# Adding shifted products on TensorE in 32 by 32 tiles instead of on GpSimd

## The chip, the cores and the metric

The kernel runs on one core of one Trainium2 chip. The metric is the device time of one execution in microseconds (us), lower is better; the median of the runs is compared. A profile is of one execution. Engines by the names of the profile: PE is TensorE, DVE is VectorE, ACT is ScalarE, POOL is GpSimd, SP issues the DMAs. PEld is PE's loading of weights.

## What is computed

An input x of 8 batches, 128 channels and 16 x 16 points, all float32, goes through two residual blocks, each after a group normalisation (groups of 4 channels over all points):

```python
x = x + L0(gn(x), w_qkv, w_gate, b_gate)      # dilated 3x3 neighbourhood attention
x = x + L1(gn(x), W_qkv, b_qkv, W_proj, b_proj)   # attention between channels
```

L0 splits q, k and v (128 channels each) into four units of 32 channels (two heads of 16), with dilations 1, 2, 4 and 8. For each point and head:

```python
kp, vp = unfold3x3(k, dil), unfold3x3(v, dil)      # nine shifted copies, zeros outside
attn = softmax(einsum('bhdn,bhdkn->bhnk', qh, kp) * scale)
out  = einsum('bhnk,bhdkn->bnhd', attn, vp)        # sum over the nine neighbours
```

Each unit's output is scaled by a gate, a softmax over the four units of a projection of the mean of each channel. L1 projects to p, takes softmax(p p^T) between the 32 channels of each of four heads over the 256 points, applies it to p, projects again and adds biases.

## The kernel before

**Halves and layout.** The eight batches are worked on in two halves (`ph` 0 and 1; batches 0, 2, 4, 6 and 1, 3, 5, 7) of four batches each. In L0 the 128 partitions of a tile hold one unit (32 channels) of all four batches of a half: partitions 32j to 32j+31 are batch j of the half. In L1, and in the input, the partitions are the 128 channels of one batch. So the result of L0 has to be brought from "one unit, four batches" into "one batch, four units". This is `restore`.

**First block.** PE projects q, k and v. DVE multiplies q by the shifted k (`multiply_qk`), PE sums over the channels of a head (`sum_scores`), DVE and ACT make the softmax, and `prob` holds the nine weights for each head and point. PE copies them to all channels of their head in `spread(ph, s, chunk)`, into two PSUM buffers in turn (banks 0 and 1, or 2 and 3): four products with 64 rows and 128 columns of weights. DVE multiplies them by the shifted v in `multiply_pv(ph, s, chunk)` and writes to `pv[s]`, nine slots of 256 points; slot 3*ci+ri belongs to column shift ci and row shift ri, slot 4 is the centre. A chunk is one column shift, in the order centre, left, right, with three row shifts each. At the image's edge a product covers fewer than 16 x 16 points: for dilation 8 a shift along one axis leaves 128 points, along both axes 64. For units 2 and 3 the centre product goes to `acc[:, ph, s, :]` instead of `pv`.

`spread` of a chunk waits until DVE has multiplied the chunk two before it (`pv_ready`), since it writes the same banks. `multiply_pv` waits for its `spread`, and in the second half for the additions of the first half's same unit to be done, since it overwrites `pv[s]`.

**Adding.** Eight additions in a tree make one sum out of a unit's nine products, in `acc` (`additions`, `operands`). POOL makes those of the first half's four units and of the second half's units 0 and 1 (`POOL_SUMS = (ND, 2)`, line 340), and counts them on `added`. DVE makes those of the second half's units 2 and 3 (`add_neighbours`, line 625), and counts on `dve_added`. POOL works its queue in the written order. Between its additions of the second half stand two roots (`rsqrt`, line 305): `rsqrt(2)` (for group 0) behind the fifth addition of unit 0, `rsqrt(3)` (for group 1) behind the first addition of unit 1. The order is in `RSQRT_AFTER`. Each waits for DVE's variance.

**Restoring and the second norm.** Batches are taken in four groups of two: groups 0 and 1 are the first half, 2 and 3 the second. `restore(g)` waits until all additions of its half are done and makes for each of two batches four products with columns of the identity: all 128 partitions in, 32 columns of weights, 256 points, one unit out to partitions 32s to 32s+31 of the bank of the batch (banks 4 and 5, 6 and 7, 0 and 1, 2 and 3 for groups 0 to 3). DVE adds x in `first_residual(g)` (line 632), which gives the channel sums too; ACT squares (`squares`), PE sums over a group of channels (`group_stats`), DVE makes the variance (`second_variance`, lines 513 to 516: `gst`, `gsq`, `gvar`), POOL the root, DVE the bias (`second_norm_bias`, line 522, `nbias`), and ACT (groups 0 and 1) or DVE (groups 2 and 3) normalises. Then comes L1, group by group.

**Order.** Each engine works through one list of calls written out by hand. Around the change PE's list is `spread` (1, 0, 0) to (1, 1, 0), `restore(0)`, `spread` (1, 1, 1), `group_stats(0)`, `restore(1)`, `spread` (1, 1, 2), `group_stats(1)` (lines 966 to 974). DVE's is (1, 0, 0) to (1, 1, 0), `first_residual(0)`, (1, 1, 1), `second_variance(0)`, `first_residual(1)`, (1, 1, 2), `second_variance(1)`, (1, 2, 0), (1, 2, 1), both biases, (1, 2, 2), (1, 3, 0), additions of unit 2, (1, 3, 1), (1, 3, 2), additions of unit 3, `attention_shift` of groups 0 and 1, `first_residual(2)` (lines 714 to 735). At the end of the second half PE runs `restore(2)` and `restore(3)` (lines 995 and 996). `keep_clock(n)` issues n products that nobody reads.

All matrix products go through the helper on line 763. One float32 product shows up in the profile as two MATMULs and two LDWEIGHTS.

Of the kernel before, what the change touches and what calls it, by code (L numbers as in the profile page):

```python
# [6 lines left out]
B, H, W = 8, 16, 16  # L7
# [23 lines left out]
NORM_ON_DVE = (2, 3)  # L31
POOL_SUMS = (ND, 2)

# [14 lines left out]
def columns(d, ci):  # L48

    co = (ci - 1) * d  # L50
    return max(0, -co), min(W, W - co), co
# [33 lines left out]
def valid_rows(s, ri):  # L85
    if PAD[s]:
        return 0, H
    ro = (ri - 1) * DIL[s]
    return max(0, -ro), min(H, H - ro)
# [8 lines left out]
def build(nc, x, wpack, consts, selc, out):  # L98
    with ExitStack() as ctx:  # L99
# [143 lines left out]
        def of_phase(ph):  # L243
            return slice(ph, B, PHASES)

        def operands(ph, s, n, target, slot):
# [245 lines left out]
        def _(dve):  # L492
# [103 lines left out]
            def multiply_pv(ph, s, chunk):  # L596
# [5 lines left out]
                dve.wait_ge(spread_ready, c + 1)  # L602
                if ph and chunk == 0:
                    dve.wait_ge(added, ADDS * (s + 1))
                c0, c1, co = columns(DIL[s], ci)
                nc_ = c1 - c0
                for n, ri, dri, r0, dr, a0, da, rows in pieces(s):
                    o = view(pv[s], (3 * ci + ri) * N + r0 * W + c0, [[dri * N + dr * W, n], [W, rows], [1, nc_]])
                    if ci == 1 and n == 1:
                        o = view(acc, (ph * ND + s) * N, [[W, rows], [1, nc_]])  # L610
                    a = view(ps, 1024 * (c % 2) + 64 * r0 + W * ri + c0, [[W * dri + 64 * dr, n], [64, rows], [1, nc_]])
                    b = view(v[s], (ph * ROWS[s] + a0) * W + c0 + co, [[da * W, n], [W, rows], [1, nc_]])
                    last = nc.vector.tensor_tensor(o, a, b, ALU.mult)  # L613
                last.then_inc(pv_ready, 1)

            def add_neighbours(ph, s):

                done = ADDS * (s - POOL_SUMS[ph])
                for n, (target, slot, after) in enumerate(additions(s)):
# [94 lines left out]
            for i in range(3):  # L714
                multiply_pv(1, 0, i)
            multiply_pv(1, 1, 0)
            first_residual(0)
            multiply_pv(1, 1, 1)
            second_variance(0)
            first_residual(1)  # L720
            multiply_pv(1, 1, 2)
# [39 lines left out]
        def _(pe):  # L761
            def mm(o, w, m, start=True, stop=True):
                return nc.tensor.matmul(o, w, m, start=start, stop=stop)  # L763
# [98 lines left out]

            def restore(g):

                ph, first = g // 2, GB * (g % 2)
                if g % 2 == 0:
                    pe.wait_ge(added, ADDS * sum(POOL_SUMS[:ph + 1]))
                    if POOL_SUMS[ph] < ND:
                        pe.wait_ge(dve_added, ADDS * (ND - POOL_SUMS[ph]))
                if ph == 0:  # L870
                    pe.wait_ge(shift_ready, g + 1)
                    pe.wait_ge(qk_ready, ND * PHASES)
                if g == 2:
                    pe.wait_ge(pv_ready, 12 * PHASES)
                for i in range(GB):
                    for s in range(ND):
                        last = mm(ps[32 * s:32 * s + 32, BANK[g] + i, 0:N],
                                  ident[:, 32 * (first + i):32 * (first + i) + 32], acc[:, ph, s, :])
                    last.then_inc(restored, 1)

# [84 lines left out]
            keep_clock(6)  # L965
            for i in range(3):
                spread(1, 0, i)
            spread(1, 1, 0)
            restore(0)
            spread(1, 1, 1)  # L970
            group_stats(0)
            restore(1)
            spread(1, 1, 2)
# [20 lines left out]
            keep_clock(3, BANK[2])  # L994
            restore(2)
            restore(3)
            fuse(0, 0)
# [65 lines left out]
```

## Time and profile before

| | us |
|---|---|
| three runs | 84.91, 84.68, 84.34 |
| median | 84.68 |
| the profiled execution's own time | 84.39 |
| its span, first to last instruction | 82.6 |

The times of a run contain the span and a constant part around it. The page gives for each engine how long it was busy and in which fortieth of the span; the chain that ended last, followed back from the last instruction; and the groups of instructions with their counts and durations. MATMULs are pipelined: a record is longer than the distance to the next one, so how long a piece of PE's work keeps the engine is read from starts, not from the sum of records. An instruction of DVE or POOL likewise overlaps the one before it by a few hundredths of a us.

### The profile page before, as it was taken

What the parts mean: (1) busy time and instruction counts of PE and PEld (TensorE: products, weight loads), DVE (VectorE), ACT (ScalarE), POOL (GpSimd) and SP (SyncE); (2) the same over time, 40 slices, a digit from 0 to 9 for tenths busy, and PEclk for the clock granted to TensorE, in tenths of its full rate; (3) what the DMA queues carried; (4) which work ended last, traced back from release to release, by engine and by line L of the source; (5) the groups of instructions that cost most, each with busy time, mean ns of one, the idle gap of its engine ahead of it and who ended that gap; (6) DMA issues with size and microseconds to landing.
All of it is one profiled execution on the core that took longest, in us unless ns stands there. A gap on an engine that the chain in (4) does not pass through costs nothing.

```text
span 82.6 us, 2228 instructions
## 1 busy us (share of the span) xinstructions
PE 67.3 (81%) x888; PEld 49.0 (59%) x888; DVE 69.6 (84%) x191; ACT 30.7 (37%) x97; POOL 42.4 (51%) x82
## 2 busy tenths in 40 slices
PE   0099899799867979999966797979999787999960
PEld 0099695476433656686855664667685545677830
DVE  1087679999999999999999698889999999857980
ACT  4396599615537000000030004220993155485320
POOL 7104279108700009999999999899990003300000
PEclk9999999999999999999999999999999999999999
DMA  0995004000000000000000000000000000011244
GB/s 5 315 356 150 1 0 100 5 0 0 8 0 0 4 12 0 0 0 0 12 0 0 0 0 0 0 8 0 0 0 0 0 8 4 0 63 64 71 158 159
DMA packets 3019, 3.11 MB, mean 38 GB/s; under 512 B 320, under 2 KB 2752, under 8 KB 3008
## 3 DMA queue, kind: packets, MB, share of 16 engines
q1 hardware_dynamic: 2576, 2.69, 9.9%
q10 hardware_dynamic: 432, 0.26, 1.4%
q8 instruction: 7, 0.11, 0.6%
q14 instruction: 4, 0.03, 0.1%
HBM read 1.91 MB, written 1.05 MB: 36 GB/s over the span
## 4 chain that ended last, share of the span: by engine, by line
DVE 42%; POOL 29%; PE 13%; issue 5%; DMA 4%; ACT 2%; POOLq 1%; ACTq 0%
DVE qk L572 17%; POOL acc L340 13%; POOL pv L340 12%; PE ps L763 11%; DVE pv L613 5%; DMA xt<-x_dram 4%; POOL rstd L305 4%; DVE acc L625 4%; DVE pv L625 3%; DVE x L632 2%; PE ps L898 2%; DVE ssum L589 1%; ACT pT L402 1%; DVE x L658 1%; POOLq L99 1%
## 5 line engine op out<-in xcount | busy, mean ns | idle before, releaser
L763 PE MATMUL ps<-prob,sel 64*128 64x192 f32 (+6 forms) x192 | 17.7, 313 | 2.9 <-DVE pv L613 1.9
L613 DVE TENSOR_TENSOR pv<-ps,v 128x128 f32<-128x128 f32 (+7 forms) x32 | 17.1, 569 | 1.7 <-PE ps L763 0.9
L763 PE MATMUL ps<-xn,wp 128*32 128x256 f32 (+1 forms) x208 | 16.4, 382 | 1.7 <-DVE shifted L582 1.2
L763 PEld LDWEIGHTS ps<-prob,sel 64*128 64x128 f32 x192 | 13.7, 186 | 6.9 <-DVE pv L613 4.8
L340 POOL TENSOR_TENSOR pv<-pv 128x240 f32<-128x240 f32 (+3 forms) x24 | 14.6, 617 | 0.1
L572 DVE TENSOR_TENSOR qk<-q,k 128x720 f32<-128x720 f32 (+7 forms) x24 | 13.9, 646 | 0.1
L763 PE MATMUL ps<-xt 128*128 128x128 f32 x56 | 10.6, 334 | 4.1 <-DMA xt<-x_dram 4.1
L763 PEld LDWEIGHTS ps<-xn,wp 128*32 128x32 f32 (+1 forms) x208 | 9.7, 116 | 6.3 <-DVE shifted L582 1.7
L340 POOL TENSOR_TENSOR acc<-acc,pv 128x256 f32<-128x256 f32 (+4 forms) x20 | 12.6, 635 | 0.5
L305 POOL TENSOR_TENSOR rstd<-gvar,mhalf 128x2 f32<-128x2 f32 (+1 forms) x6 | 4.9, 824 | 14.9 <-DVE gvar L516 14.9
L763 PEld LDWEIGHTS ps<-xt 128*128 128x128 f32 x56 | 8.6, 230 | 5.2 <-DMA xt<-x_dram 4.1
L763 PE MATMUL ps<-qk,cs 128*32 128x192 f32 (+6 forms) x176 | 7.8, 302 | 0.9 <-ACT v L385 0.5
L340 POOL TENSOR_TENSOR acc<-pv 128x256 f32<-128x256 f32 x4 | 2.9, 728 | 8.5 <-DVE pv L613 8.5
L395 ACT ACTIVATE expd<-shifted 128x576 f32<-128x576 f32 x2 | 1.4, 684 | 15.8 <-DVE shifted L582 15.8
L402 ACT ACTIVATE pT<-x 128x256 f32<-128x256 f32 x8 | 3.3, 411 | 10.4 <-DVE x L632 10.4
L763 PEld LDWEIGHTS ps<-qk,cs 128*32 128x32 f32 x176 | 4.7, 109 | 3.6 <-ACT v L385 1.0
L541 DVE TENSOR_REDUCE sums<-xt 128x1 f32<-128x256 f32 x8 | 2.8, 413 | 2.8 <-DMA xt<-x_dram 2.8
L763 PE MATMUL ps<-p,mT 128*128 128x256 f32 x16 | 4.6, 399 | 0.3 <-ACT mT L429 0.2
L763 PE MATMUL ps<-acc,cs 128*32 128x256 f32 x64 | 4.1, 383 | 0.7 <-issue 0.6
L360 ACT ACTIVATE xn<-xt 128x256 f32<-128x256 f32 x8 | 3.2, 404 | 2.0 <-DMA xt<-x_dram 2.0
L415 ACT ACTIVATE p<-ps,wp 128x256 f32<-128x256 f32 x8 | 3.4, 473 | 1.1 <-PE ps L763 1.1
L572 DVE TENSOR_TENSOR qk<-ps,k 128x128 f32<-128x128 f32 (+4 forms) x12 | 3.8, 379 | 0.0
(75 smaller groups left out, 94.0 us busy)
## 6 DMA issues: line engine op xcount, KB each, us to landing
xt<-x_dram SPq DMA_DIRECT2D x4, 256.0 KB, 3.6
out_dram<-x SPq DMA_DIRECT2D x8, 128.0 KB, 1.8
wp<-wpack_dram SPq DMA_DIRECT2D x1, 325.0 KB, 5.6
sel<-selc_dram SPq DMA_DIRECT2D x4, 64.0 KB, 3.9
cs<-consts_dram ACTq DMA_DIRECT2D x1, 130.0 KB, 3.3
cs<-consts_dram ACTq DMA_DIRECT2D x2, 64.0 KB, 2.6
```

Of the source, the lines that this page charges most:

```text
L305: nc.gpsimd.tensor_tensor(rstd[:, bs], gvar[:, bs], mhalf[:, bs], ALU.pow).then_inc(rstd_ready, 1)
L340: nc.gpsimd.tensor_tensor(o, a, b, ALU.add).then_inc(added, 1)
L360: nc.scalar.activation(xn1[:, b // GB, b % GB, :], xt[:, b, :], ACT.Square, accum_out=sums[:, b, 1:2]).then_inc(square_ready, 1)
L402: nc.scalar.activation(pT[:, g, 2 * i:2 * i + 2, :].rearrange("p t n -> p (t n)"), x1[:, b, :], ACT.Square, accum_out=sums1[:, b, 1:2]).th ...
L415: nc.scalar.activation(p1[:, g, i, :], ps[:, BANK[g] + i, 0:N], ACT.Identity, bias=wp[:, W_B1:W_B1 + 1]).then_inc(p1_copied, 1)
L541: nc.vector.tensor_reduce(sums[:, b, 0:1], xt[:, b, :], AX.X, ALU.add).then_inc(sum_ready, 1)
L572: last = nc.vector.tensor_tensor(o, a, b, ALU.mult)
L613: last = nc.vector.tensor_tensor(o, a, b, ALU.mult)
L625: nc.vector.tensor_tensor(o, a, b, ALU.add).then_inc(dve_added, 1)
L632: nc.vector.scalar_tensor_tensor(out=x1[:, b, :], in0=ps[:, BANK[g] + i, 0:N], scalar=1.0, in1=xt[:, b, :], op0=ALU.mult, op1=ALU.add, acc ...
L763: return nc.tensor.matmul(o, w, m, start=start, stop=stop)
L898: last = nc.tensor.transpose(ps[:, BANK[g] + i, P * t:P * t + P], p1[:, g, i, P * t:P * t + P], ident)
```

## The change

`POOL_SUMS` becomes (3, 2) and `TENSOR_SUMS = ((3,), ())`: nobody adds the first half's unit 3 in SBUF any more. `restore` is replaced by `sum_units(ph, units)`. It works in tiles of 32 rows and 32 columns: for each unit s and each batch j of the half, the product of a 32 x 32 identity with partitions 32j to 32j+31 goes to partitions 32s to 32s+31 of the bank of batch j. For a unit that is already added that is one product of 256 points for each batch, from `acc`. For the first half's unit 3 it is nine for each batch, one for each neighbour straight from `pv[3]`, over the points that the neighbour covers, accumulated in PSUM. All four banks of a half are filled by one call; `restored` counts a batch when its last unit in the order of issue has its last product.

PE's list has `sum_units(0, (3,))` between `spread` (1, 0, 1) and (1, 0, 2), `sum_units(0, (0, 1, 2))` behind (1, 0, 2), then `spread` (1, 1, 0) and (1, 1, 1), `group_stats(0)`, `spread` (1, 1, 2), `group_stats(1)`; and for the second half `sum_units(1, (0, 1, 2, 3))` in place of the two `restore`. DVE's list has `first_residual(0)` ahead of (1, 1, 0) and `first_residual(1)` ahead of (1, 1, 1). The first half's unit 3 has its centre product in `pv[3]`, and the second half's multiply of unit 3 waits for all four batches to be restored.

```diff
--- before.py
+++ after.py
@@ -29,7 +29,8 @@
 GROUPS = B // GB
 NORM_ON_ACT = (4, 6, 1, 3, 5, 7)
 NORM_ON_DVE = (2, 3)
-POOL_SUMS = (ND, 2)
+POOL_SUMS = (3, 2)
+TENSOR_SUMS = ((3,), ())
 
 RSQRT_AFTER = ((1, 0, 4), (1, 1, 0))
 
@@ -243,6 +244,15 @@
         def of_phase(ph):
             return slice(ph, B, PHASES)
 
+        def neighbours(s):
+
+            return [(3 * ci + ri, *valid_rows(s, ri), *columns(DIL[s], ci)[:2])
+                    for ci in CENTRE_FIRST for ri in CENTRE_FIRST]
+
+        def added_before(ph, s):
+
+            return len([u for u in range(POOL_SUMS[ph], s) if u not in TENSOR_SUMS[ph]])
+
         def operands(ph, s, n, target, slot):
 
             ci, ri = divmod(slot, 3)
@@ -600,13 +610,15 @@
                 if chunk == 0:
                     dve.wait_ge(proj_copied, tiles.index((2, s, ph)) + 1)
                 dve.wait_ge(spread_ready, c + 1)
-                if ph and chunk == 0:
+                if ph and chunk == 0 and s in TENSOR_SUMS[0]:
+                    dve.wait_ge(restored, SLOTS)
+                elif ph and chunk == 0:
                     dve.wait_ge(added, ADDS * (s + 1))
                 c0, c1, co = columns(DIL[s], ci)
                 nc_ = c1 - c0
                 for n, ri, dri, r0, dr, a0, da, rows in pieces(s):
                     o = view(pv[s], (3 * ci + ri) * N + r0 * W + c0, [[dri * N + dr * W, n], [W, rows], [1, nc_]])
-                    if ci == 1 and n == 1:
+                    if ci == 1 and n == 1 and s not in TENSOR_SUMS[ph]:
                         o = view(acc, (ph * ND + s) * N, [[W, rows], [1, nc_]])
                     a = view(ps, 1024 * (c % 2) + 64 * r0 + W * ri + c0, [[W * dri + 64 * dr, n], [64, rows], [1, nc_]])
                     b = view(v[s], (ph * ROWS[s] + a0) * W + c0 + co, [[da * W, n], [W, rows], [1, nc_]])
@@ -615,7 +627,7 @@
 
             def add_neighbours(ph, s):
 
-                done = ADDS * (s - POOL_SUMS[ph])
+                done = ADDS * added_before(ph, s)
                 for n, (target, slot, after) in enumerate(additions(s)):
                     if n == 0 or ADD_NEEDS[n] > ADD_NEEDS[n - 1]:
                         dve.wait_ge(pv_ready, 12 * ph + 3 * s + ADD_NEEDS[n])
@@ -713,11 +725,11 @@
             multiply_pv(0, 3, 2)
             for i in range(3):
                 multiply_pv(1, 0, i)
+            first_residual(0)
             multiply_pv(1, 1, 0)
-            first_residual(0)
+            first_residual(1)
             multiply_pv(1, 1, 1)
             second_variance(0)
-            first_residual(1)
             multiply_pv(1, 1, 2)
             second_variance(1)
             for i in range(2):
@@ -860,23 +872,37 @@
                     last = mm(o, sel[half:half + 64, j % 2, s, :], m)
                 last.then_inc(spread_ready, 1)
 
-            def restore(g):
-
-                ph, first = g // 2, GB * (g % 2)
-                if g % 2 == 0:
-                    pe.wait_ge(added, ADDS * sum(POOL_SUMS[:ph + 1]))
-                    if POOL_SUMS[ph] < ND:
-                        pe.wait_ge(dve_added, ADDS * (ND - POOL_SUMS[ph]))
+            def sum_units(ph, units):
+
                 if ph == 0:
-                    pe.wait_ge(shift_ready, g + 1)
+                    pe.wait_ge(shift_ready, PHASES)
                     pe.wait_ge(qk_ready, ND * PHASES)
-                if g == 2:
+                else:
                     pe.wait_ge(pv_ready, 12 * PHASES)
-                for i in range(GB):
-                    for s in range(ND):
-                        last = mm(ps[32 * s:32 * s + 32, BANK[g] + i, 0:N],
-                                  ident[:, 32 * (first + i):32 * (first + i) + 32], acc[:, ph, s, :])
-                    last.then_inc(restored, 1)
+                parts = []
+                for s in units:
+                    if s in TENSOR_SUMS[ph]:
+                        pe.wait_ge(pv_ready, 12 * ph + 3 * s + 3)
+                        parts.append([(pv[s], slot * N, r0, r1, c0, c1) for slot, r0, r1, c0, c1 in neighbours(s)])
+                        continue
+                    if s < POOL_SUMS[ph]:
+                        pe.wait_ge(added, ADDS * (sum(POOL_SUMS[:ph]) + s + 1))
+                    else:
+                        pe.wait_ge(dve_added, ADDS * (added_before(ph, s) + 1))
+                    parts.append([(acc, (ph * ND + s) * N, 0, H, 0, W)])
+                for n in range(max(len(part) for part in parts)):
+                    for s, part in zip(units, parts):
+                        if n >= len(part):
+                            continue
+                        t, offset, r0, r1, c0, c1 = part[n]
+                        dims = [[W, r1 - r0], [1, c1 - c0]]
+                        for j in range(SLOTS):
+                            rows = slice(32 * j, 32 * j + 32)
+                            last = mm(view(ps, 512 * (BANK[2 * ph] + j) + r0 * W + c0, dims, 32 * s, 32),
+                                      ident[rows, rows], view(t, offset + r0 * W + c0, dims, 32 * j, 32),
+                                      start=(n == 0), stop=(n == len(part) - 1))
+                            if s == (2, 3)[ph]:
+                                last.then_inc(restored, 1)
 
             def group_stats(g):
                 pe.wait_ge(sum_ready, B + GB * (g + 1))
@@ -963,13 +989,14 @@
             keep_clock(2)
             spread(0, 3, 2)
             keep_clock(6)
-            for i in range(3):
+            for i in range(2):
                 spread(1, 0, i)
-            spread(1, 1, 0)
-            restore(0)
-            spread(1, 1, 1)
+            sum_units(0, (3,))
+            spread(1, 0, 2)
+            sum_units(0, (0, 1, 2))
+            for i in range(2):
+                spread(1, 1, i)
             group_stats(0)
-            restore(1)
             spread(1, 1, 2)
             group_stats(1)
             for i in range(2):
@@ -992,8 +1019,7 @@
             attention(1)
             pe.wait_ge(pv_ready, 12 * PHASES)
             keep_clock(3, BANK[2])
-            restore(2)
-            restore(3)
+            sum_units(1, (0, 1, 2, 3))
             fuse(0, 0)
             group_stats(2)
             finish(0, 0)
```

## Rows read from the trace of the kernel before

**Rows 1.** The page: the span, and each engine's busy time, share and instructions
```profile
span 82.6 us, 2228 instructions
PE 67.3 (81%) x888; PEld 49.0 (59%) x888; DVE 69.6 (84%) x191; ACT 30.7 (37%) x97; POOL 42.4 (51%) x82
```

**Rows 2.** The chain that ended last, in time: start us, us, what
```profile
31.66 0.70 POOL pv L340
...
49.31 0.96 DVE pv L613
...
52.90 0.71 POOL rstd L305
```

**Rows 3.** Table by windows: stretch, its us, each engine busy (instructions), PEclk, DMA share, GB/s
```profile
50.00:57.00 7.00, 5.90 (x70) 4.22 (x64) 6.27 (x21) 1.82 (x8) 6.63 (x10) 1.00 0.01 2
57.00:65.40 8.40, 7.69 (x118) 5.54 (x115) 8.28 (x28) 4.85 (x12) 4.80 (x8) 1.00 0.00 0
61.00:65.40 4.40, 3.73 (x91) 2.89 (x90) 4.33 (x19) 1.62 (x5) 0.80 (x2) 1.00 0.00 0
```

**Rows 4.** Timeline of DVE, 48 to 58: start, us, what, [idle before and its releaser]
```profile
48.40 0.91 DVE L613 TENSOR_TENSOR pv<-ps,v 128x720 f32<-128x720 f32 x1 [0.17 <-PE ps L763]
...
50.18 0.41 DVE L632 SCALAR_TENSOR_TENSOR x<-ps,xt 128x256 f32<-128x256 f32 x1
...
51.20 0.86 DVE L613 TENSOR_TENSOR pv<-ps,v 128x672 f32<-128x672 f32 x1 [0.25 <-PE ps L763]
52.09 0.16 DVE L513 TENSOR_TENSOR gst<-ps,signs 128x4 f32<-128x4 f32 x1
52.28 0.34 DVE L515 TENSOR_TENSOR gsq<-gst 128x2 f32<-128x2 f32 x1
...
53.87 0.86 DVE L613 TENSOR_TENSOR pv<-ps,v 128x672 f32<-128x672 f32 x1 [0.32 <-PE ps L763]
...
57.08 0.72 DVE L522 TENSOR_TENSOR nbias<-gst,rstd 128x2 f32<-128x2 f32 x2
```

**Rows 5.** Timeline of POOL: unit 3's first and last addition, later additions, second root
```profile
46.34 0.45 POOL L340 TENSOR_TENSOR acc<-acc,pv 128x128 f32<-128x128 f32 x1
...
48.80 0.46 POOL L340 TENSOR_TENSOR acc<-acc,pv 128x128 f32<-128x128 f32 x1
...
51.24 1.36 POOL L340 TENSOR_TENSOR pv<-pv 128x240 f32<-128x240 f32 x2
...
56.36 0.70 POOL L305 TENSOR_TENSOR rstd<-gvar,mhalf 128x2 f32<-128x2 f32 x1
```

**Rows 6.** Timeline of PE, 46 to 51: spread, restore(0) and spread
```profile
46.49 0.47 PE L763 MATMUL ps<-prob,sel 64*128 64x180 f32 x4
...
47.47 0.88 PE L763 MATMUL ps<-prob,sel 64*128 64x180 f32 x8 [0.51 <-DVE pv L613]
...
49.31 1.07 PE L763 MATMUL ps<-acc,cs 128*32 128x256 f32 x16
...
49.98 0.40 PE L763 MATMUL ps<-acc,cs 128*32 128x256 f32 x4
50.31 0.41 PE L763 MATMUL ps<-prob,sel 64*128 64x168 f32 x2
```

**Rows 7.** Timeline of PE: a spread of few columns, and products of 32 columns
```profile
42.46 0.66 PE L763 MATMUL ps<-prob,sel 64*128 64x64 f32 x8 [0.69 <-DVE pv L613]
...
73.80 0.48 PE L763 MATMUL ps<-pT 128*32 128x32 f32 x32
```

**Rows 8.** Timeline of DVE: additions of the second half's unit 2, one shape
```profile
60.52 0.83 DVE L625 TENSOR_TENSOR acc<-acc,pv 128x192 f32<-128x192 f32 x1
...
62.18 0.35 DVE L625 TENSOR_TENSOR acc<-acc,pv 128x192 f32<-128x192 f32 x1
```

**Rows 9.** Timeline of PE and DVE: the second half's restore, and the first residual behind it
```profile
65.51 1.93 PE L763 MATMUL ps<-acc,cs 128*32 128x256 f32 x32 [0.58 <-issue]
66.21 0.42 DVE L632 SCALAR_TENSOR_TENSOR x<-ps,xt 128x256 f32<-128x256 f32 x1
```

## What the change will do to the time

> **What bounds the kernel now.** The profiled execution took 84.39 us, of which 82.6 us are the span and 1.79 us lie around it; the median of the three timed runs is 84.68 us. I read the page first, for who is busy: VectorE leads with 84% of the span, PE has 81%, GpSimd 51% [rows 1]. Then the chain of waits in order of time [rows 2]. From 31.66 us on it is GpSimd, adding the nine neighbours of the first half's four units one after another, up to 49.26. At 49.31 it passes to VectorE, and it leaves it again for a reciprocal root of GpSimd at 52.90.
>
> A chain that runs through GpSimd tempts one to say that GpSimd bounds this stretch. So I asked the table by windows how much VectorE was idle beside it [rows 3]: 6.27 of 7.00 us busy from 50 to 57, 8.28 of 8.40 from 57 to 65.4, at the full granted clock. VectorE is the bound there as well; the two end nearly together. What faster restoring can win here is at most VectorE's idle time, and its timeline shows where that lies [rows 4] (I write (half, unit, chunk) for `multiply_pv` and `spread`): 0.17 us before the multiply of (1, 0, 2) at 48.40, and 0.25 at 51.20 and 0.32 at 53.87, where `spread` had stood behind `restore` on PE. In all 0.74 us.
>
> **The change part by part.**
>
> *GpSimd.* Unit 3's eight additions go. They run from 46.34 to 49.26, 2.9 us [rows 5]. The second half's additions can then begin when (1, 0, 0) is multiplied, about 2 us sooner. But the sixth still stands behind `rsqrt(2)` on the queue, and that root waits for the variance of group 0, which VectorE makes. So GpSimd's gain turns into a wait for VectorE, unless that variance comes earlier too.
>
> *PE, unit 3.* In place of the additions come 9 neighbours x 4 batches = 36 products in 32x32 tiles, two MATMULs each; columns per batch 256 + 4 x 128 + 4 x 64 = 1024. Price of a column: `restore(0)` makes its 8 products of 256 columns, four side by side, in 1.07 us, of which the last MATMULs' 0.40 holds 0.19 beyond their own 0.21: (1.07-0.19)/4 = 0.22 us for one pass, 0.43 us for both [rows 6]. `spread` shows that two row groups also run side by side: eight MATMULs of 180 columns in 0.88 us, 0.69 without the tail, where one after another they would need 8 x 180/256 x 0.215 = 1.2 us [rows 6]. Unit 3's four batches are four row tiles of one column tile. If all four overlap: 1024/256 x 0.43 = 1.71 us, the lower bound, since one tile's nine neighbours are a sequence. Upper bound, none overlap: 4 x 1.71 = 6.8 us. Between lies the loading of weights: eight MATMULs of 64 columns in `spread`, with 128 weight columns, took 0.66 us, some 0.25 more than their columns ask; with 32 weight columns, 32 MATMULs of 32 columns took 0.48 us [rows 7], which is columns (32 x 0.027/4 = 0.21) and tail. I take 1.8 us, near the lower bound, because each kind of overlap that it needs is in a row. A change between the array's shapes costs 0.12 us: the last pass of `restore(0)` starts at 49.98, takes 0.21, and `spread` starts at 50.31 [rows 6].
>
> This piece stands between `spread` (1, 0, 1) and (1, 0, 2). Its own wait, for (0, 3, 2), is over before. The last record of `spread` (1, 0, 1) ends at 46.96 [rows 6], so PE can take new work at about 46.79. PE now waits from there to 47.47 for a free bank, so 0.68 us of the piece are hidden. The rest isn't: start 46.91, end 48.71, `spread` (1, 0, 2) at 48.83 instead of 47.47. VectorE waits for that: its multiply begins 0.93 us behind (47.47 to 48.40 now), at 49.76. **First term: +1.36 us** (+1.27 to +6.4).
>
> *VectorE's order.* Both `first_residual(0)` and `first_residual(1)` now stand ahead of the variance of group 0; before, one did. From rows 4 and 2, start to start: (1, 0, 2) 0.83 (its 0.91 less the 0.08 by which neighbours overlap), a residual pair 0.77 (50.18 to 50.95), (1, 1, 0) 0.87, a pair 0.77, (1, 1, 1) 0.78; sum 4.02 us. Before it was 52.09-48.40 = 3.69, stalls included. **Second term: +0.33 us.** In this stretch PE restores units 0 to 2, 12 products on 12 different tiles: 0.43 us if all overlap, 1.3 if four do. With two changes of shape `spread` (1, 1, 0) then starts at 50.1 or 51.0 and can be read at 51.0 or 51.9, while VectorE asks at 51.36: nothing, or +0.55. I take nothing, as tiles of other columns and of other rows overlap in rows 6. The centre of unit 3 goes to `pv` instead of `acc` at the same size, and the multiply (1, 3, 0) waits for a `restored` that is eight us old: both nothing.
>
> *A block that goes.* The variance's second step takes 0.34 us at 52.28, under a GpSimd addition that ends at 52.60; the step before it takes 0.16 [rows 4, 5]. GpSimd will be idle then. **Third term: -0.18 us** (0 to -0.18).
>
> *What is late next.* `rsqrt(2)` starts at 52.90+1.36+0.33-0.18 = 54.41. From there to the end of the root of group 1 GpSimd needs 57.06-52.90 = 4.16 us (root, three additions, the first of unit 1, root) with hardly a hole [rows 2, 5], so the second root is there at 58.57 instead of 57.06. Would VectorE be there? It came to `second_norm_bias(0)` 57.08-52.09 = 4.99 us after that variance began; without the residual pair (0.77), the stall (0.32) and the block (0.18) that is 3.72 us, from 53.78 on: 57.5. So it waits for the second root for about 1 us and leaves at 59.3 instead of 57.8. Behind that wait are (1, 2, 2), (1, 3, 0) to (1, 3, 2) and 16 additions, all without a hole [rows 3], so the full 1.5 us go through to 65.4. ACT's normalisations and PE's second projections, behind the same biases, end before VectorE.
>
> *The second half's restore.* 16 products on 16 tiles instead of four by four. Nobody waits for it now: it starts at 65.51, VectorE shifts the attention until 66.20 and takes the first residual at 66.21 [rows 9]. All four batches come near the end, at 65.51+0.43+0.19 = 66.1: 0. With overlap of four only, the first is there at 67.3: +1.1 us. I take 0, and no gain, since the residuals have no stall to lose.
>
> Sum: 1.36+0.33-0.18 = **+1.5 us**; 84.39+1.5 = 85.9 for an execution like the profiled one, which lies 0.29 under the median, so 86.2 against 84.68.
>
> **A rule beside the rows.** An addition of VectorE takes 0.83 us at 60.52 while GpSimd adds, and the same shape 0.35 at 62.18, when GpSimd has finished [rows 8]. The Trainium skill, SBUF — State Buffer, "Who interferes with whom", says: a VectorE instruction with two SBUF inputs and a GpSimd instruction that reads SBUF exclude each other, and the later one waits. By that rule the trace agrees, and it speaks for a gain that I don't forecast: rival 3.
>
> **The rivals.**
> 1. *Small products are slower than their columns.* Place: unit 3 on PE. If row tiles of one column tile don't overlap, 6.8 instead of 1.8 us: +5.0 more, 91.2. If PE can't issue its 144 instructions in 1.8 us but only at the mean pace of the window 61 to 65.4 (181 in 4.4 us [rows 3]), 3.5 us: +1.7 more, 87.9. Against: 32 MATMULs with their weight loads in 0.48 us [rows 7], but nothing shows four row tiles. Chance 0.13. The Trainium skill, TensorE: Matmul & The Clock Gate, "Wait — 56ns, not 53.3ns?", gives about 62 ns per MATMUL where instructions are decoded by the sequencer's firmware; that would be an estimated 4.5 us for these 72. Rows 7, at 15 ns each, speak against it here.
> 2. *Only VectorE's own delay counts*, because the second root is there in time. VectorE would leave the biases at 57.8 to 58.3 instead of 57.8: 0 to +0.5, or 84.7 to 85.2. It decides if GpSimd gives the root by 57.8, which needs its 4.16 us of work to shrink to 3.4. Against: no hole in them. Chance 0.17.
> 3. *Faster.* Place: VectorE's additions of unit (1, 2), four of which are 0.4 us longer beside GpSimd, 1.6 in all. If GpSimd, 2.9 us ahead, is through with them first, that time is won: 83.1. It decides if `rsqrt(2)` starts before about 51 us. Against: VectorE's new order makes that variance later, not sooner. Chance 0.10.
>
> **How the numbers follow.** The forecast has 0.60; its own terms (unit 3 in 1.7 to 2.2 us, the +0.55, the block) make 85.9 to 87.3. The range goes down to rival 2's end, 84.6, and up to 88.2, which takes in rival 1's milder half; outside are rival 3 (0.10) and the other half (0.07). A measurement of this kernel can tell about 1% from no change. Faster by over 1% (under 83.8): 0.09. Slower by over 1% (over 85.5), forecast and rival 1: 0.73. Within: 0.18.
>
> **What would show it.** After the change: `spread` (1, 0, 2) starts near 48.8 and VectorE idles 1.3 us before that multiply; unit 3's products span 1.7 to 2.2 us; GpSimd idles about 3 us before `rsqrt(2)`, which starts near 54.4; VectorE idles about 1 us before the bias of group 1, released by GpSimd; `attention_shift(0)` starts near 66.8, and what follows takes as long as before. I am wrong if the products span much more, if that root starts by 53, or if VectorE's additions of unit (1, 2) take 0.35 us each.

## The result, and the profile after

The changed kernel takes 88.0 us (median of four runs, 87.07 to 89.49) against 84.8 us: ratio 1.0357, 95% interval 1.0302 to 1.0412. The ratio and its interval, here and below, leave out executions more than 1.5% above the fastest of their kernel, here 89.49 us and one of 85.76 us of the kernel before. The change is slower, and by twice what I forecast: +3.2 us by the medians, +3.0 by the ratio, instead of +1.5. The profiled execution took 87.07 us with a span of 85.3, so 2.7 us of span are there to be found. The mean granted clock was 0.956 and 0.960 in the two shorter executions and 0.941 and 0.942 in the two longer ones.

The page of the changed kernel: the span, the engines' busy time and share, and TensorE's granted clock in tenths over 40 slices of 2.1 us:

```profile
span 85.3 us, 2350 instructions
PE 68.5 (80%) x952; PEld 52.2 (61%) x952; DVE 69.6 (82%) x191; ACT 30.8 (36%) x97; POOL 40.1 (47%) x74
PEclk9999999999999999999999999999999855599998
```

VectorE's busy time is that of [rows 1], GpSimd's is 2.3 us shorter. The new thing stands in the clock's line: 9 tenths or more until slice 31, then one slice at 8 and three at 5. The same line of the kernel before:

```profile
PEclk9999999999999999999999999999999999999999
```

I had used that clock for every duration and never asked what the change would do to it.

**The first half.** PE's timeline of the changed kernel (start, us, what), answering to [rows 6]:

```profile
46.83 1.96 PE L775 MATMUL ps<-pv,cs 32*32 32x256 f32 x72
48.72 0.88 PE L775 MATMUL ps<-prob,sel 64*128 64x180 f32 x8
49.53 0.69 PE L775 MATMUL ps<-acc,cs 32*32 32x256 f32 x24
50.15 1.49 PE L775 MATMUL ps<-prob,sel 64*128 64x192 f32 x16
```

Unit 3's 72 MATMULs start at 46.83 and the next `spread` at 48.72: 1.77 us for them and 0.12 for the change of shape (forecast: 46.91, 1.8, 48.83). The four row tiles of one column tile do overlap, and units 0 to 2 take 0.62 us with the change of shape. VectorE's timeline, answering to [rows 4]:

```profile
49.64 0.91 DVE L625 TENSOR_TENSOR pv<-ps,v 128x720 f32<-128x720 f32 x1 [1.48 <-PE ps L775]
...
53.50 0.15 DVE L523 TENSOR_TENSOR gst<-ps,signs 128x4 f32<-128x4 f32 x1
53.68 0.16 DVE L525 TENSOR_TENSOR gsq<-gst 128x2 f32<-128x2 f32 x1
...
54.91 0.61 DVE L525 TENSOR_TENSOR gsq<-gst 128x2 f32<-128x2 f32 x1
...
57.53 0.14 DVE L532 TENSOR_TENSOR nbias<-gst,rstd 128x2 f32<-128x2 f32 x1
58.33 0.63 DVE L532 TENSOR_TENSOR nbias<-gst,rstd 128x2 f32<-128x2 f32 x1 [0.66 <-POOL rstd L315]
...
66.44 0.22 DVE L651 TENSOR_REDUCE amax<-ps 128x2 f32<-128x64 f32 x1
```

The multiply of (1, 0, 2) waits 1.48 us for PE where it waited 0.17. The second bias waits 0.66 us for GpSimd's root. `attention_shift(0)` begins at 66.44 instead of 65.33. GpSimd's timeline shows the wait that its gain became, 2.78 us, and 4.18 us from there to the end of the second root:

```profile
54.12 0.71 POOL L315 TENSOR_TENSOR rstd<-gvar,mhalf 128x2 f32<-128x2 f32 x1 [2.78 <-DVE gvar L526]
...
57.59 0.71 POOL L315 TENSOR_TENSOR rstd<-gvar,mhalf 128x2 f32<-128x2 f32 x1
```

**The second half.** From `attention_shift(0)` to the end of the span the kernel before needed 82.6-65.33 = 17.3 us, the changed one 85.3-66.44 = 18.9. PE's timeline of that stretch, answering to [rows 9] (first the kernel before, then the changed one), VectorE's first residual, and the table by windows of the changed kernel (stretch, its us, busy time of each engine, granted clock, DMA):

```profile
67.85 0.49 PE L763 MATMUL ps<-wp,ablk 128*128 128x128 f32 x2 [0.40 <-DVE ablk L649]
...
68.69 0.70 PE L763 MATMUL ps<-p,mT 128*128 128x256 f32 x2 [0.23 <-ACT mT L429]
```

```profile
66.67 0.73 PE L775 MATMUL ps<-acc,cs 32*32 32x256 f32 x32 [0.63 <-DVE acc L637]
69.07 0.80 PE L775 MATMUL ps<-wp,ablk 128*128 128x128 f32 x2 [1.67 <-DVE ablk L661]
...
70.22 1.22 PE L775 MATMUL ps<-p,mT 128*128 128x256 f32 x2
```

```profile
67.51 0.42 DVE L644 SCALAR_TENSOR_TENSOR x<-ps,xt 128x256 f32<-128x256 f32 x1 [0.20 <-PE ps L775]
```

```profile
67.00:67.50 0.50, 0.40 (x32) 0.00 (x0) 0.28 (x2) 0.21 (x1) 0.00 (x0) 1.00 0.00 0
67.50:68.00 0.50, 0.00 (x0) 0.00 (x0) 0.49 (x3) 0.02 (x1) 0.00 (x0) 0.59 0.00 0
68.00:68.50 0.50, 0.00 (x0) 0.00 (x0) 0.47 (x4) 0.50 (x3) 0.00 (x0) 0.50 0.00 0
...
74.00:75.00 1.00, 1.00 (x6) 0.83 (x5) 0.89 (x3) 0.26 (x1) 0.00 (x0) 0.79 0.00 0
```

The sum in tiles is through in 0.73 us where `restore(2)` and `restore(3)` took 1.93 [rows 9]. PE then has nothing to do for 1.67 us until VectorE delivers `ablk`; the kernel before had 0.4 us there. In this gap the granted clock falls to 0.50 (1.2 GHz), and stays there until about 74.4. The same pair of MATMULs with `ablk` that took 0.49 us before takes 0.80, the pair with `mT` 1.22 instead of 0.70. This stretch is on the chain that ended last (start, us, what):

```profile
69.07 0.81 PE ps L775 x2
...
70.22 5.35 PE ps L775 x18
```

The Trainium skill, TensorE: Matmul & The Clock Gate, "HAM oscillation — how this bites in real kernels", tells of a kernel whose bursts of products are separated by waits for a DMA, each of which brings the clock back to half. This trace agrees in that the clock fell in a wait; but here the wait was for VectorE and 1.67 us long, shorter than the waits of the page's example, so the page alone would not have told me that this one suffices. I should still have weighed it, for the change shortens PE's work just ahead of a wait.

### The profile page after: what moved, and what is told of

Read it like the earlier page. It is cut to its first block, busy times and chain, and to the rows that moved or that the text cites. A ratio compares the mean times of both kernels' runs of the same rounds, so it can differ in the third digit from the quotient of the medians.

```text
span 85.3 us, 2350 instructions
## 1 busy us (share of the span) xinstructions
PE 68.5 (80%) x952; PEld 52.2 (61%) x952; DVE 69.6 (82%) x191; ACT 30.8 (36%) x97; POOL 40.1 (47%) x74
## 4 chain that ended last, share of the span: by engine, by line
DVE 51%; PE 31%; POOL 5%; issue 4%; DMA 4%; ACT 2%; ACTq 0%
PE ps L775 30%; DVE qk L582 20%; DVE pv L625 12%; DMA xt<-x_dram 4%; DVE acc L637 4%; DVE pv L637 3%; DVE ssum L599 3%; POOL acc L350 2%; DVE x L644 2%; DVE smax L589 2%; POOL rstd L315 2%; PE ps L924 2%; DVE srec L600 1%; DVE prob L602 1%; DVE x L670 1%
## 5 line engine op out<-in xcount | busy, mean ns | idle before, releaser
L625 DVE TENSOR_TENSOR pv<-ps,v 128x128 f32<-128x128 f32 (+7 forms) x33 | 17.3, 563 | 2.5 <-PE ps L775 1.6
L350 POOL TENSOR_TENSOR pv<-pv 128x240 f32<-128x240 f32 (+2 forms) x20 | 13.6, 691 | 0.5 <-DVE pv L625 0.3
L775 PEld LDWEIGHTS ps<-xn,wp 128*32 128x32 f32 (+1 forms) x208 | 10.9, 119 | 4.7 <-DVE shifted L592 1.7
L315 POOL TENSOR_TENSOR rstd<-gvar,mhalf 128x2 f32<-128x2 f32 (+1 forms) x6 | 4.9, 825 | 17.3 <-DVE gvar L526 17.3
L350 POOL TENSOR_TENSOR acc<-acc,pv 128x256 f32<-128x256 f32 (+3 forms) x16 | 11.0, 691 | 0.4
L775 PE MATMUL ps<-p,mT 128*128 128x256 f32 x16 | 5.5, 460 | 0.2
L775 PE MATMUL ps<-wp,ablk 128*128 128x128 f32 x16 | 3.9, 382 | 1.7 <-DVE ablk L661 1.7
L775 PEld LDWEIGHTS ps<-wp,ablk 128*128 128x128 f32 x16 | 3.0, 258 | 2.4 <-DVE ablk L661 2.3
L419 ACT ACTIVATE xn<-x,nbias,rstd 128x256 f32<-128x256 f32 x4 | 2.2, 592 | 4.5 <-DVE nbias L532 4.5
```

The source lines that it names most:

```text
L315: nc.gpsimd.tensor_tensor(rstd[:, bs], gvar[:, bs], mhalf[:, bs], ALU.pow).then_inc(rstd_ready, 1)
L350: nc.gpsimd.tensor_tensor(o, a, b, ALU.add).then_inc(added, 1)
L419: nc.scalar.activation(xn1[:, g, i, :], x1[:, b, :], ACT.Identity, bias=nbias[:, b:b + 1], scale=rstd[:, b:b + 1]).then_inc(xn1_act_ready, 1)
```

## The experiments

Two theories for the 1.6 us behind 66.4: T1, the second half's tiles leave PE idle and the clock falls; T2, the first half's delay makes the idle time.

**The two parts apart.** First, the changed kernel with its second half restored as before:

```diff
-            sum_units(1, (0, 1, 2, 3))
+            restore(2)
+            restore(3)
```

> The changed kernel with the second half restored as before, in 128x32 tiles four by four. Theory T1 (the granted clock falls because the second half's sum in 32x32 tiles keeps PE busy for 0.7 us only where restore kept it busy for 1.9, with 1.7 us of idle time behind it): the clock stays at 1.00 throughout, and only the delay in VectorE's order is left, +1.1 us against the kernel before (the shift seen at attention_shift(0), 66.44 against 65.33). Rival T2 (the clock falls because the first half's new work makes VectorE late, so that PE is idle from 64.0 to 65.1 before the kept products): the clock still falls at about 67.5, and the time stays near +2.7 us.

Measured: 86.07 us against 84.84, ratio 1.0172 (1.0092 to 1.0253). The profiled execution shows the clock at 9 tenths or more in 39 slices and at 7 in the last, with a mean of 0.994; one of the other three has a mean of 0.98. PE was idle for 0.84 and 0.58 us ahead of the restore, and the clock held:

```profile
66.55 0.94 PE L775 MATMUL ps<-xt 128*128 128x128 f32 x6 [0.84 <-DVE pv L625]
...
68.07 1.93 PE L775 MATMUL ps<-acc,cs 128*32 128x256 f32 x32 [0.58 <-issue]
```

Then the kernel before with `restore(2)` and `restore(3)` replaced by the 16 products in tiles, and nothing else:

> The kernel before with one part of the change alone: the second half's 16 products in 32x32 tiles. T1: the granted clock falls to half behind them, near 66.5, and the time is +1.5 us or somewhat more. T2: nothing falls, and the time is within 0.3 us of before. What I predicted for this part was 0.

Measured: 86.52 us against 84.84, ratio 1.0203 (1.0130 to 1.0276). Its mean clock is 0.959 to 0.978 in the four executions. Its page shows the fall by itself, PE's timeline the same gap, and the table by windows the moment:

```profile
PEclk9999999999999999999999999999999955599999
```

```profile
65.69 0.73 PE L763 MATMUL ps<-acc,cs 32*32 32x256 f32 x32 [0.62 <-DVE acc L625]
68.08 0.80 PE L763 MATMUL ps<-wp,ablk 128*128 128x128 f32 x2 [1.66 <-DVE ablk L649]
```

```profile
67.00:68.00 1.00, 0.00 (x0) 0.00 (x0) 0.93 (x6) 1.00 (x5) 0.00 (x0) 0.88 0.00 0
```

T1 holds, T2 falls. By the medians the parts cost +1.2 and +1.7 us, together 2.9 of the 3.2.

**Is it the clock alone?** The changed kernel, and the kernel before with the second half's tiles, each with more unread products around the sum (the edit of the first; in the second, `sum_second()` stands where `sum_units` does):

```diff
-            keep_clock(3, BANK[2])
+            keep_clock(6, BANK[2])
             sum_units(1, (0, 1, 2, 3))
+            pe.wait_ge(ashift_ready, 2)
+            keep_clock(6)
```

> The changed kernel with PE kept busy around the second half's sum: six instead of three unread products ahead of it, and six more behind it once the attention's shift has been read. If the lost time behind 66.4 is the clock's alone, the clock stays at 1.00 and the time is +1.1 to +1.3 us against before, like that of the kernel whose second half is restored as before. If something else in the tiles costs time there (the residual's late start, 0.2 us seen), it stays above that by as much. If the fall is decided by the products' form and not by idle time, the clock falls all the same, and it stays near +2.7.

> The kernel before with the second half's 16 products in 32x32 tiles, and PE kept busy around them by 128x128 products (six ahead instead of three, six behind). The tiles alone cost 1.7 us, with the clock at half from about 67 to 73 us. If that is all the clock, it stays at 1.00 here and the time is that of the kernel before plus the 0.2 us by which the first residual waits: 0 to +0.4 us. If the tiles cost time in another way, it stays above +1 us at full clock.

Measured: 85.81 us against 84.84 (1.0131, 1.0063 to 1.0200), the value of the kernel with the second half as before; and 84.53 against 84.46 (1.0025, 0.9993 to 1.0057). The mean granted clock was 0.994 to 1.00 in every execution. With the clock held, the tiles of the second half cost nothing, as I had priced them without asking for the clock. The 0.2 us of the residual's wait can't be told from nothing.

**Is it the 32x32 form?** The changed kernel with unread work in 32x32 tiles, meant to last as long as the 128x128 products did:

> The changed kernel with PE kept busy around the second half's sum for as long as in the kernel whose kept products are 128x128 (1.28 us ahead and 1.28 us behind), but with unread products in 32x32 tiles, 48 of 256 columns each time. If what lets the clock fall is only that PE stands idle there, the clock stays at 1.00 and the time is +1.0 to +1.3 us against before. If products in 32x32 tiles hold it less well than 128x128 ones of the same duration, it falls all the same, and the time stays near +3 us.

Measured: 87.22 us against 84.53 (1.0324, 1.0260 to 1.0388), with the clock at 1.00 in all four executions. So the form alone does not let the clock fall; whether it holds it as well as 128x128 products of the same duration was not measured, since these lasted longer. Neither expected time came, since the unread products took longer than I had given them. PE's timeline:

```profile
66.16 2.09 PE L775 MATMUL ps<-xt,cs 32*32 32x256 f32 x94 [0.84 <-DVE pv L625]
...
68.56 1.55 PE L775 MATMUL ps<-xt,cs 32*32 32x256 f32 x54
70.28 1.28 PE L775 MATMUL ps<-xt,cs 32*32 32x256 f32 x39 [0.17 <-issue]
71.49 0.49 PE L775 MATMUL ps<-wp,ablk 128*128 128x128 f32 x2
```

The first 94 MATMULs need (2.09-0.19)/94 = 0.020 us each, where 16 tiles at 256 columns would allow 0.21/16 = 0.013; those of the second lot need (1.55-0.19)/54 = 0.025 and (1.28-0.19)/39 = 0.028. The sum had to stand behind the first lot, so that the residual waited 0.55 us instead of 0.2; and the product with `ablk` stood behind the second until 71.49, though `ablk` was there at about 70.4. The two delays, 0.35 and 1.0 us, make up 1.4 of the 1.7 us by which this kernel lies above the one with 128x128 products.

What sets the moment of the fall stays open. The idle time ahead of the sum is not enough by itself: the changed kernel with `restore` has it too and held the clock. The length of the gap behind it is not the whole either: the clock is at 0.50 from 67.6 in the changed kernel, 0.2 us into the gap, and from 67.8 in the kernel with the second half's tiles only, 1.3 us into it.

**The second term, VectorE's order.** The changed kernel with the variance of group 0 ahead of `first_residual(1)`:

```diff
             multiply_pv(1, 1, 0)
-            first_residual(1)
             multiply_pv(1, 1, 1)
             second_variance(0)
+            first_residual(1)
```

> The changed kernel with VectorE's variance of group 0 put back ahead of first_residual(1), as before. Theory of the second term: rsqrt(2) starts 0.8 us sooner (53.3 instead of 54.1), GpSimd's second root is there by 57.5 and VectorE no longer waits for it (0.66 us in the changed kernel), so attention_shift(0) starts 0.5 to 0.8 us sooner and the time falls by as much, if the clock behaves the same. Rival: VectorE's own work is the bound, the wait only moves (to the second variance, whose steps already meet GpSimd's additions), and the gain is under 0.2 us.

Measured: 87.49 us against 84.84, ratio 1.0304, where the changed kernel has 1.0357; the intervals overlap. The clock falls as in the changed kernel, so the profile decides. VectorE needs 46.77 to 66.22 from the start of (1, 0, 0) to `attention_shift(0)`, 19.45 us, against 46.39 to 66.44, 20.05: 0.6 us less, and no wait before either bias. The theory's amount came in the profile; the times themselves don't tell it from nothing.

**The first term, unit 3's place.** From here on the second half is restored as before. Unit 3's products are split: those of its first two chunks stand where PE had six unread products, those of the last behind `spread` (1, 0, 1):

```diff
-            keep_clock(6)
+            sum_first_chunks()
             for i in range(2):
                 spread(1, 0, i)
-            sum_units(0, (3,))
+            sum_last_chunk()
```

> The changed kernel with its second half restored as before, and with unit 3's 36 products split: the 24 of its first two chunks (768 of 1024 columns, about 1.3 us) where PE had six unread products before the softmax of the second half is ready, and only the last 12 (256 columns, 0.43 us) between spread (1, 0, 1) and (1, 0, 2). Theory of the first term (the 1.3 us by which unit 3's products hold back one spread): VectorE's idle time before the multiply of (1, 0, 2) falls from 1.48 us to 0.3 or less, the whole second half moves forward by 1.1 to 1.3 us, and the time is within 0.4 us of the kernel before. Rival: the delay returns, since GpSimd's second root stands between the halves; then the gain against the kernel with the whole unit in one piece is under 0.5 us. A granted clock that falls near 44 us, with the unread products gone, would spoil it.

Measured: 84.43 us against 84.53 (0.9991, 0.9948 to 1.0033). The 1.2 us of the first half are gone. Three of the twelve executions, at 85.1 to 85.3 us, have a mean clock of 0.973 to 0.977; where it fell in them is not known, and the profiled one is at 9 tenths or more in every slice. Timelines of PE and of VectorE:

```profile
43.59 1.51 PE L775 MATMUL ps<-pv,cs 32*32 32x256 f32 x48
...
47.43 0.64 PE L775 MATMUL ps<-pv,cs 32*32 32x128 f32 x24
48.01 0.88 PE L775 MATMUL ps<-prob,sel 64*128 64x180 f32 x8
```

```profile
48.94 0.91 DVE L625 TENSOR_TENSOR pv<-ps,v 128x720 f32<-128x720 f32 x1 [0.17 <-PE ps L775]
...
57.62 0.63 DVE L532 TENSOR_TENSOR nbias<-gst,rstd 128x2 f32<-128x2 f32 x1 [0.66 <-POOL rstd L315]
```

The wait for PE is 0.17 us again, as in [rows 4]. The wait for GpSimd's root is still there, as the chain of 4.16 us on GpSimd says.

**The root's place on GpSimd.** `RSQRT_AFTER = ((1, 0, 7), (1, 1, 0))` instead of `((1, 0, 4), (1, 1, 0))`:

> The changed kernel with its second half restored as before and rsqrt(2) behind the eighth instead of the fifth addition of unit 0 on GpSimd's queue. Theory: GpSimd's 2.8 us of idle time before that root take in the three additions, so the second root comes about 2 us after the first (instead of 3.5) and is there before VectorE asks; VectorE's 0.65 us of waiting go, GpSimd is through 1 to 2 us sooner, and the additions of unit (1, 2) get shorter by 0.4 us for each that now finds GpSimd done. Together 0.7 to 1.5 us under the kernel with the roots as they were (which was +1.2 against before). Rival: VectorE's blocked steps of the two variances grow by what the wait loses, and the gain is under 0.3.

Measured: 84.18 us against 84.53 (0.9963, 0.9927 to 0.9999), so 1.6 us under the kernel with the root as it was (+1.23 there, -0.35 here), a little more than expected. GpSimd's and VectorE's timelines:

```profile
54.99 0.71 POOL L315 TENSOR_TENSOR rstd<-gvar,mhalf 128x2 f32<-128x2 f32 x1 [0.69 <-DVE gvar L526]
55.66 0.73 POOL L350 TENSOR_TENSOR acc<-pv 128x256 f32<-128x256 f32 x1
56.68 0.71 POOL L315 TENSOR_TENSOR rstd<-gvar,mhalf 128x2 f32<-128x2 f32 x1 [0.29 <-DVE gvar L526]
```

```profile
57.98 0.76 DVE L532 TENSOR_TENSOR nbias<-gst,rstd 128x2 f32<-128x2 f32 x2
...
61.48 0.34 DVE L637 TENSOR_TENSOR acc<-acc,pv 128x192 f32<-128x192 f32 x1
```

GpSimd's idle time of 2.78 us before the first root is 0.69. VectorE waits for neither root, and an addition that took 0.83 us in [rows 8] takes 0.34. One of the twelve executions, 85.99 us at a mean clock of 0.959, is not in the ratio. This is my rival 3 in small: GpSimd's lead is worth something, if the root isn't put in front of it.

**Both edits together.** First both edits, then both with six unread products ahead of `restore(2)`, then both again beside these:

> Both edits together: unit 3's products split over PE's free time, and rsqrt(2) later on GpSimd's queue, with the second half restored as before. If the first term, the wait for the root and the two engines' exclusion are what the first half's part of the change costs, this kernel is faster than before by 0.5 to 1.5 us. If the two edits remove the same wait, it is no better than the better of them alone.

> The kernel with both edits (unit 3 split, rsqrt(2) later, second half restored as before) and six instead of three unread products ahead of restore(2). In some executions of it without them the mean granted clock was 0.94 to 0.96 and the time 2 to 4 us longer. If that is the same fall of the clock around the second half's restore, more work on PE there removes these executions, and the median is 83.2 to 84.0, 0.5 to 1.3 us under before. If the fall has another place, such executions remain.

> Both edits again, beside the kernel with more unread products on the same chip: 0.4 to 1.2 us under before, with some executions at a lower clock if the cause is as said there.

Some executions have a lower mean clock, so each is given, its mean clock in brackets. First run of both edits: 83.20 (1.00), 84.03 (1.00), 84.02 (1.00), 85.46 (0.959), 87.11 (0.939), 83.31 (1.00); ratio of the four at 1.00, 0.9888 (0.9826 to 0.9950). Second run, on another chip: 83.15 (1.00) and 84.83 (1.00), and four from 85.53 to 86.39 at 0.959 or 0.960; median 85.65 against 84.46, so not better than before as it stands. With six unread products ahead of `restore(2)`: 87.65 (0.934), 83.17, 86.20 (0.960), 84.36, 83.28, 83.27 (0.994 to 1.00), median 83.82 against 84.46. So more work on PE ahead of `restore(2)` did not remove such executions. In the profiled execution of this last kernel, the one of 87.65 us, the clock fell elsewhere, as its table by windows and PE's timeline show:

```profile
53.00:54.00 1.00, 0.50 (x8) 0.31 (x4) 0.97 (x3) 0.00 (x0) 0.71 (x2) 1.00 0.00 0
54.00:54.50 0.50, 0.26 (x2) 0.26 (x4) 0.47 (x3) 0.00 (x0) 0.50 (x2) 0.59 0.00 0
54.50:55.00 0.50, 0.50 (x6) 0.50 (x8) 0.47 (x2) 0.00 (x0) 0.40 (x1) 0.50 0.00 0
...
64.00:66.00 2.00, 2.00 (x52) 1.53 (x50) 1.02 (x5) 1.25 (x4) 0.00 (x0) 0.92 0.04 8
```

```profile
54.24 1.27 PE L775 MATMUL ps<-prob,sel 64*128 64x96 f32 x8 [0.74 <-DVE pv L625]
```

It fell in the idle 0.74 us ahead of `spread` (1, 2, 1), not ahead of (1, 2, 0) as the expectation below has it. In the profiled execution of the second run of both edits, 85.53 us, the same gap of 0.75 us ended at 54.11, and the clock fell at about 55.2, while PE worked on unread products:

```profile
55.00:55.50 0.50, 0.50 (x4) 0.30 (x3) 0.50 (x2) 0.00 (x0) 0.44 (x1) 0.73 0.00 0
```

So I gave PE more work around there:

```diff
             spread(1, 1, 2)
+            keep_clock(2, BANK[0] + 1)
             group_stats(1)
+            keep_clock(3, BANK[1] + 1)
```

> The kernel with both edits and six unread products ahead of restore(2), and five more between spread (1, 1, 2) and (1, 2, 0), two ahead of group_stats(1) and three behind it, where PE stood idle for 0.2 and 0.75 us. Where the granted clock fell in the two kernels without these, it fell at about 54.5 us, behind that idle time. If that is its place, no execution falls any more, and the median is 83.2 to 83.8, 0.7 to 1.3 us under before. If it still falls, in some executions, the median lies between 84 and 86 and the place is another.

Measured: 83.80, 83.62, 83.76, 83.69, 83.27 us at 0.999 to 1.00, and one of 90.53 us at a mean clock of 0.784; median 83.73 against 84.43, ratio of the five 0.9874 (0.9816 to 0.9931). By the median that is 0.7 us under the kernel before and 4.3 us under the changed one. The mean of all six is 84.8 us, though, and that of the kernel before in the same run 84.7: one execution in six takes the gain back. PE's gap ahead of `spread` (1, 2, 1) is gone in the profile. That the five products keep the clock up is not shown: one execution of six fell with them, eight of eighteen without (both edits twice, and with six products), too few to tell apart. A mean of 0.784 over 88.7 us is some 38 us at half clock ((1-0.784) x 2 x 88.7, an estimate), far more than in any profiled execution; why is open, since its profile wasn't taken.

How long VectorE takes from the start of (1, 0, 0) to `attention_shift(0)`, from the profiled executions:

| kernel | from | to | us |
|---|---|---|---|
| before | 46.46 | 65.33 | 18.87 |
| second half's tiles only | 46.57 | 65.47 | 18.90 |
| changed | 46.39 | 66.44 | 20.05 |
| changed, second half as before | 47.86 | 67.88 | 20.02 |
| changed, variance first | 46.77 | 66.22 | 19.45 |
| unit 3 split | 46.99 | 65.71 | 18.72 |
| root later | 47.26 | 65.80 | 18.54 |
| both | 46.39 | 64.15 | 17.76 |

## Why the prediction was half right

**Right: the direction, and the mechanism of the first half, step by step.** First term forecast +1.36, found 49.64-48.40 = +1.24. Second term forecast +0.33, found (53.50-49.64)-3.69 = +0.17: the residual pairs took 0.70 and 0.69 us, not 0.77 each. Third term -0.18, found: the second step took 0.16. But the block did not go, it moved to group 1: the second step of its variance, 0.16 us at 54.84 before, takes 0.61 at 54.91. So VectorE needed 4.03 us from the first variance to the biases and not 3.72, and that it came at 57.53 where I had forecast 57.5 is luck, since the variance began 0.28 us earlier than forecast. GpSimd's chain between the roots forecast 4.16, found 4.18. It started at 54.12 (forecast 54.41) and ended at 58.30 (forecast 58.57). The wait before the second bias forecast 1, found 0.66. `attention_shift(0)` was 1.11 us later instead of 1.5. The part by itself, with the second half as before, costs 1.2 us.

**Right: PE's price in tiles.** Of the bounds 1.71 to 6.8 us the lower one held, 1.77, and I had placed the 12 products of units 0 to 2 rightly in VectorE's shadow. Rival 1 fell.

**Wrong: "The second half's restore ... I take 0".** This is the step that failed. It asked who waits for the products and found nobody; the first residual waits 0.20 us, which is small. It didn't ask what PE's shorter work does to PE. The term is +1.7 us when made alone, nearly all of it the granted clock: with the clock held the same tiles cost 0.07 us, which the interval doesn't tell from 0. The idle time was to be had from the forecast's own numbers: the sum was to end at 66.1, and the product with `ablk` starts at 67.85 in the kernel before, when VectorE has made `ablk`; so 0.4 us of gap become 1.7. The kernel's own text was the hint: `keep_clock(3, BANK[2])`, three unread products, stands ahead of that restore. My sum carried the clock of the kernel before into a stretch where the change takes away PE's work. That 88.0 us still lies inside my range of 84.6 to 88.2 is luck: its upper end was made for rival 1, products slower than their columns, which did not happen.

**Rivals 2 and 3** didn't happen as such, but rival 3 marked a place where time was to be won. Splitting unit 3's products gave 1.3 us back; moving the root, with those products in one piece, gave 1.6.

## What to carry to other kernels

When a change makes PE faster ahead of a wait, add up PE's idle time behind it and price the stretch at both levels of the clock: here the 1.2 us that PE saved cost 1.7. When work leaves an engine's queue, look at what stands in front of the rest of that queue; the gain ends at the first instruction that waits for somebody else, so move that one too. And a piece that PE can begin early (six of nine neighbours were ready some 3 us before the last three) is better split over PE's idle time than put in one block ahead of what the busiest engine waits for.

## What the runs showed of the hardware

- Four row tiles of one column tile overlap in float32: 36 products with 4 x 1024 columns in 1.77 us, 0.06 us more than the columns of one row tile alone ask (1.71, an estimate from [rows 6]).
- The first 94 MATMULs of a long run in 32x32 tiles go at 0.020 us each (1.9 us), the later ones at 0.025 to 0.028, while 32 that had been waiting for a semaphore were through at (0.73-0.40)/31 = 0.011 us each. The Trainium skill, TensorE: Matmul & The Clock Gate, "Wait — 56ns, not 53.3ns?", gives about 25 ns as the least distance between starts; 0.020 and 0.011 lie below it, and the measurement decides. The columns would ask 0.013 each, so a long sum over 16 tiles of 256 columns seems bound by its instructions; no run was made to show it.
- The clock fell to 0.50 in a gap of 1.67 us of PE and stayed there for 6.8 us, from 67.6 to 74.4, through stretches in which PE was busy without a hole. In the profiled execution with both edits and six unread products it stayed at half from 54.1 to 64.3, 10.2 us. The mean clocks of the changed kernel fit the same two lengths: (1-0.960) x 2 x 85.9 = 6.9 us, (1-0.942) x 2 x 87.7 = 10.2 us (estimates). With both edits the clock fell in a gap of 0.74 us in one profiled execution and 1.1 us behind one of 0.75 us in another; it did so in some executions and not in others, on the same code.
- With unread products in 32x32 tiles, 1.9 us of them ahead of the sum and 2.8 behind it, the clock stayed at 1.00 in four executions of four.
